# Transformer layers on one core: context loads ahead of weight stores, statistics moved a stage earlier, and a rounding shared with ScalarE

## What is computed

```python
x = x + _L0_ffn_ref(_layernorm(x, axis=-1), ...)            # 16 routed experts and a shared one
x = x + _L1_xattn_ref(_layernorm(x, axis=-1), ctx_2048, ...)  # attention, q and output in 8-bit steps
x = x + _L1_ffn_ref(_layernorm(x, axis=-1), gate_cp, up_cp, down_cp)
x = x + _L2_xattn_ref(_layernorm(x, axis=-1), ...)
x = x + _L2_ffn_ref(_layernorm(x, axis=-1), gate_w, up_w, down_w)

def _L1_ffn_ref(...):    # weights interpolated from control points
    w = 0.5 * (2.0 * p1 + (p2 - p0) * f + (...) * f2 + (...) * f3)
    inter = jax.nn.silu(gate) * up

def _mx_dequant(t):      # of L2_ffn, for activations and for each weight
    scales = jnp.maximum(max_abs / 448.0, 1e-30)              # per block of 32
    q = (blocks / scales[..., None]).astype(jnp.float8_e4m3fn).astype(jnp.float32)
    return (q * scales[..., None]).reshape(rows, feat)
```

## Time and profile before

| | |
|---|---|
| median of 3 runs | 2426.94 us (2417.49 to 2431.23) |
| profiled execution | 2430.76 us, span 2428.9 us |
| TensorE matmul busy | 2241.5 us (92% of the span) |
| VectorE / ScalarE / GpSimd busy | 1312.8 / 772.9 / 776.6 us |
| granted TensorE clock, mean | 0.954 |
| experts / second attention | about 684 to 956.6 / 956.7 to 1328.0 us |
| spline / column stage | 1328.0 to 1385.9 / 1385.9 to 1536.3 us |

### The profile page before, as it was taken

The page is one execution under the profiler, slowest core; times in us unless marked ns, Lnnn a source line. Parts: engine busy times, 40 slices in busy tenths (PEclk is TensorE's granted clock), DMA queues, the critical chain, the costliest instruction groups (busy, mean ns, idle before and its releaser), DMA issues. The chain is left out here.

```text
span 2428.9 us, 29430 instructions
## 1 busy us (share of the span) xinstructions
PE 2241.5 (92%) x10009; PEld 1185.2 (49%) x10009; DVE 1312.8 (54%) x3424; ACT 772.9 (32%) x2045; POOL 776.6 (32%) x784
## 2 busy tenths in 40 slices
PE   8999999998999997888886898799998899999899
PEld 4455555555455654444443454534443444444454
DVE  5544344106217656545555475776663355555897
ACT  1134344314011112434444311511110456645433
POOL 3655455203203214432232332400000365656100
PEclk9999999998999998989988799999999899999899
DMA  7025300005276864121111641520001211211000
GB/s 198 1 82 187 124 17 13 1 1 165 72 291 249 298 224 155 50 73 50 58 35 41 217 148 52 200 92 5 9 5 55 81 48 51 61 39 43 20 14 15
DMA packets 99802, 214.80 MB, mean 88 GB/s; under 512 B 19332, under 2 KB 40228, under 8 KB 97736
## 3 DMA queue, kind: packets, MB, share of 16 engines
q1 hardware_dynamic: 92232, 195.61, 23.7%
q0 software_dynamic: 7424, 17.32, 2.5%
HBM read 156.75 MB, written 51.18 MB: 86 GB/s over the span
## 5 line engine op out<-in xcount | busy, mean ns | idle before, releaser
L3864 POOL TENSOR_SCALAR a_p<-a_p,a_li 100x257 f32<-100x257 f32 x252 | 187.9, 763 | 110.7 <-DVE a_li L3727 110.7
L634 POOL TENSOR_SCALAR a_shared<-a_shared,a_li 128x361 f32<-128x361 f32 x104 | 131.5, 1265 | 182.4 <-DVE a_li L542 182.4
L3482 PE MATMUL bank<-l_early,a_ctx 128*128 128x512 f32 (+1 forms) x384 | 180.2, 615 | 0.0
L1590 PE MATMUL bank<-w_ctx,w_wk 128*128 128x361 f32 x256 | 101.6, 548 | 30.4 <-DMA w_ctx<-in_ctxT 29.8
L3482 PEld LDWEIGHTS bank<-l_early,a_ctx 128*128 128x128 f32 (+1 forms) x384 | 68.9, 189 | 85.0 <-issue 85.0
L314 PE MATMUL bank<-a_wk,a_ctx 128*128 128x512 f32 (+1 forms) x192 | 95.0, 615 | 9.6 <-DMA a_wk<-in_L_xattn_Wk 6.2
L2688 POOL TENSOR_TENSOR e_v<-e_triple,e_inv 128x768 f32<-128x768 f32 x20 | 33.1, 1654 | 206.7 <-DVE e_inv L2665 206.7
L692 ACT ACTIVATE a_shared<-a_shared,a_nm 128x361 f32<-128x361 f32 x104 | 62.1, 597 | 99.0 <-DVE a_nm L536 99.0
L2768 PE MATMUL bank<-f_h,s_w 128*128 128x400 f32 x256 | 92.1, 514 | 0.0
L314 PE MATMUL bank<-a_wv,a_ctx 128*128 128x512 f32 (+1 forms) x192 | 90.7, 592 | 0.0
L2418 ACT ACTIVATE f_sg<-bank 128x512 f32<-128x512 f32 x25 | 14.9, 597 | 237.4 <-PE bank L2201 221.7
(11 more groups left out here) (492 smaller groups left out, 4890.4 us busy)
## 6 DMA issues: line engine op xcount, KB each, us to landing
slots_x<-zero SPq DMA_DIRECT2D x4, 4096.0 KB, 27.0
s_whole<-in_L_ffn_w SPq DMA_DIRECT2D x24, 512.0 KB, 3.6
e_wg<-in_L_ffn_w_gate SPq DMA_DIRECT2D x16, 704.0 KB, 6.6
e_wu<-in_L_ffn_w_up SPq DMA_DIRECT2D x16, 704.0 KB, 8.2
e_wd<-in_L_ffn_w_down SPq DMA_DIRECT2D x16, 512.0 KB, 4.2
e_xg<-slots_x SPq DMA_DIRECT2D x16, 512.0 KB, 5.3
slots_y<-e_y SPq DMA_DIRECT2D x32, 256.0 KB, 4.5
a_ctx<-in_ctxT SPq DMA_DIRECT2D x30, 256.0 KB, 3.2
```

What stands on the lines that cost most here:

```text
L634: pool.tensor_scalar(p[s % NP], p[s % NP], li[:, b % 2, h:h + 1], None, ALU.mult).then_inc(normed, 1)
L1590: mm = nc.tensor.matmul(R.bank("k", b, n)[:, 0:T], wks[:, kc, n * P:(n + 1) * P], cx[b % 2][:, kc, :], start=(kc == 0), stop=(kc == KC - 1))
L3482: mm = nc.tensor.matmul(bank[0:m, :], columns[:, kc], w[:, kc, :], start=(kc == 0), stop=(kc == KC - 1))
L3864: pool.tensor_scalar(p[g % 2][j][:, lo:hi], p[g % 2][j][:, lo:hi], li[:, h, i:i + 1], None, ALU.mult) \
```

## The change

Four parts. In the second attention SP loads context and mask of b before it stores the spline weights of b - 2 and loads the taps of b; and the statistics that the spline stage needs are taken there, by VectorE behind each `add_output`, with the roots by GpSimd two sequences later (the last two in the spline stage). In the spline stage VectorE normalises all eight sequences first, into eight buffers; TensorE transposes four of them before the control point products and four behind them, with other banks. The experts round nine triples and the column stage seven, with three buffers, and not at n = 7. In the rounding VectorE masks the exponent ahead of the next half's scales (`power`), ScalarE makes of it the constant by a Relu with scale and bias (`lift`), and VectorE adds and subtracts in two scalar_tensor_tensor, which put back the offset.

```diff
+RAISE = 1.5 * 2.0 ** 20
...
-        self.half = self.sb("half", [P, 1])
+        self.half, self.lowest = self.sb("half", [P, 1]), self.sb("lowest", [P, 1])
...
@@ stage_L0_experts @@
-                triples.store(sp, EARLY_TRIPLES - 1)
...
                     copy_mid(u)
                     if u + 2 < U:
                         copy_x(u + 2)
+                    if u in ROUNDING_UNITS:
+                        triples.lift(act, ROUNDING_UNITS.index(u))
...
                         n = ROUNDING_UNITS.index(u)
+                        triples.power(dve, n)
                         if n + 1 < triples.n:
                             triples.scales(dve, step, n + 1)
                         triples.rounding(dve, step, n)
@@ stage_L1_attention @@
                 for b in range(2, B):
-                    store_weights(b - 2)
-                    load_taps(b)
                     sp.wait_ge(*R.full("v", b - 2, 2))
                     sp.wait_ge(multiplied, b - 1)
                     sp.dma_start(cx[b % 2][:], ctxT[b]).then_inc(c_in[b % 2], 16)
                     sp.wait_ge(maxed, (b - 1) * NH)
                     sp.dma_start(m_in[b % 2][:], mask[b]).then_inc(mk_in[b % 2], 16)
+                    store_weights(b - 2)
+                    load_taps(b)
...
+                def measure_next(b):
+                    step(dve.bn_stats(k.next_stats[:, b, :], k.res[:, b, :]))
+                    step(dve.bn_aggr(k.next_stat[:, b, :], k.next_stats[:, b, :]))
+                    dve.tensor_scalar(k.next_var[:, b:b + 1], k.next_stat[:, b, 1:2], LN_EPS, None, ALU.add) \
+                        .then_inc(next_var_made, 1)
...
                     if before:
                         add_output(b - 1)
+                        measure_next(b - 1)
...
                 add_output(B - 1)
+                measure_next(B - 1)
...
+                def next_root(b):
+                    pool.wait_ge(next_var_made, b + 1)
+                    pool.tensor_tensor(k.next_rstd[:, b:b + 1], k.next_var[:, b:b + 1], k.half[0:S, :], ALU.pow)
...
                     interpolate(b)
+                    if b >= 2:
+                        next_root(b - 2)
@@ constants @@
-EARLY_TRIPLES = 10
-ROUNDING_UNITS = [*range(4, 16), *range(24, 32)]
-STORES_AFTER = {t + 3 if t < 6 else t + 7: t for t in range(EARLY_TRIPLES - 1)}
+EARLY_TRIPLES = 9
+ROUNDING_UNITS = [*range(4, 16), *range(24, 30)]
+COLUMN_ROUNDINGS = [n for n in range(FC - 1) if n != FC // 2 - 1]
+STORES_AFTER = {t + 3 if t < 6 else t + 7: t for t in range(EARLY_TRIPLES)}
@@ class Triples @@
+    def power(self, dve, n):
+        dve.wait_ge(self.scaled, n + 1)
+        dve.tensor_scalar(self.c[n % 2][:].bitcast(I32), self.v[n % 2][:].bitcast(I32), EXPONENT, None, ALU.bitwise_and) \
+            .then_inc(self.power_taken, 1)
+
     def rounding(self, dve, step, n):
-        dve.wait_ge(self.scaled, n + 1)
+        dve.wait_ge(self.power_lifted, n + 1)
         a, p = self.v[n % 2][:], self.c[n % 2][:]
-        step(dve.tensor_scalar(p.bitcast(I32), a.bitcast(I32), EXPONENT, None, ALU.bitwise_and))
-        step(dve.tensor_scalar(p, p, 2.0 ** -6, 1.5 * 2.0 ** 20, ALU.max, ALU.mult))
-        step(dve.tensor_tensor(a, a, p, ALU.add))
-        dve.tensor_tensor(a, a, p, ALU.subtract).then_inc(self.v_rounded, 1)
+        step(dve.scalar_tensor_tensor(a, p, RAISE * 2.0 ** -6, a, ALU.add, ALU.add))
+        dve.scalar_tensor_tensor(a, a, RAISE * 2.0 ** -6, p, ALU.subtract, ALU.subtract).then_inc(self.v_rounded, 1)
+
+    def lift(self, act, n):
+        act.wait_ge(self.power_taken, n + 1)
+        p = self.c[n % 2][:]
+        act.activation(p, p, ACT.Relu, bias=self.k.lowest[:, 0:1], scale=RAISE).then_inc(self.power_lifted, 1)
@@ stage_columns_ffn @@
-        triples = Triples(k, ctx, tag, raw, rounded, EARLY_TRIPLES, FC, 2)
+        triples = Triples(k, ctx, tag, raw, rounded, EARLY_TRIPLES, FC, 3)
...
+                def gates(lo, hi):
+                    for m in range(lo, hi):
+                        silu(m)
+                        if (m - 3) / 2 in COLUMN_ROUNDINGS:
+                            triples.lift(act, COLUMN_ROUNDINGS.index((m - 3) // 2))
...
-                    if n < triples.n:
-                        if n + 1 < triples.n:
-                            triples.scales(dve, step, n + 1)
-                        triples.rounding(dve, step, n)
+                    if n in COLUMN_ROUNDINGS:
+                        i = COLUMN_ROUNDINGS.index(n)
+                        triples.power(dve, i)
+                        if i + 1 < triples.n:
+                            triples.scales(dve, step, i + 1)
+                        triples.rounding(dve, step, i)
@@ stage_L1_ffn @@
-            xn = [sb(f"xn{i}", [S, D]) for i in range(2)]
+            xn = [sb(f"xn{i}", [S, D]) for i in range(B)]
...
+            x_bank, sum_bank = lambda b: k.bank[(b + GB) % B], lambda half, v: k.bank[(QUADS * (half + 1) + v) % B]
...
+                    for b in range(GB):
+                        turn(b)
                     pe.wait_ge(c_in, 16)
                     for t in range(PARTS_W):
                         pe.wait_ge(multiplied, t + 1)
...
+                    for b in range(GB, B):
+                        pe.wait_ge(laid, (PARTS_W - 1) * N + b - GB + 1)
+                        turn(b)
                     pe.wait_ge(basis_in, 16)
                     for half in range(2):
+                        pe.wait_ge(xT_made, GB * (half + 1))
                         for v in range(QUADS):
-                            pe.wait_ge(xT_made, GB * (half + 1))
+                            if half == 0:
+                                pe.wait_ge(w_made, (PARTS_W - 1) * N + v + 1)
...
-                    for t in range(PARTS_W):
-                        measure(2 * t)
-                        measure(2 * t + 1)
-                        beyond_border(t)
                     for b in range(B):
                         normalize(b)
+                    for t in range(PARTS_W):
+                        beyond_border(t)
```

More of the change, by code:

```diff
@@ L553, in _ @@
                 dve.memset(k.ones[:], 1.0)
+                dve.memset(k.lowest[:], -RAISE * 2.0 ** -6)
                 dve.memset(k.res[:, B], 0.0)
@@ L2721, in _ @@
             def _(sp):
-                for t in range(2):
+                for t in range(3):
                     triples.load(sp, t)
@@ L2728, in _ @@
                     triples.stored(sp, t)
-                    if t + 2 < FC - EARLY_TRIPLES:
-                        triples.load(sp, t + 2)
+                    if t + 3 < FC - EARLY_TRIPLES:
+                        triples.load(sp, t + 3)
                 sp.wait_ge(early_in, 6 * 16)
@@ L2961, in _ @@
                 def _(pool):
-                    def root(b):
-                        pool.wait_ge(var_made, b + 1)
-                        pool.tensor_tensor(rstd[:, b:b + 1], var[:, b:b + 1], k.half[0:S, :], ALU.pow).then_inc(rstd_made, 1)
+                    pool.tensor_tensor(k.next_rstd[:, B - 2:B], k.next_var[:, B - 2:B], k.half[0:S, :].to_broadcast([S, 2]), ALU.pow) \
+                        .then_inc(rstd_made, 1)
                     for t in range(PARTS_W):
@@ L2978, in _, with turn @@
                 def _(pe):
+                    def turn(b):
+                        pe.wait_ge(xn_made, b + 1)
+                        for v in range(QUADS):
+                            mm = nc.tensor.transpose(x_bank(b)[:, v * S:(v + 1) * S], xn[b][:, v * P:(v + 1) * P], k.ident[0:S, 0:S])
+                        mm.then_inc(x_turned, 1)
+                    for b in range(GB):
+                        turn(b)
                     pe.wait_ge(c_in, 16)
@@ L2981, in _ @@
                         pe.wait_ge(multiplied, t + 1)
-                        for side, emptied in ((0, laid), (1, w_made)):
+                        for side in range(2):
                             for n in range(N):
                                 if t > 0:
-                                    pe.wait_ge(emptied, (t - 1) * N + n + 1)
+                                    pe.wait_ge((laid, w_made)[side], (t - 1) * N + n + 1)
+                                elif side == 1:
+                                    pe.wait_ge(xT_made, n + 1)
                                 rows = slice(32 * n, 32 * n + TERMS)
@@ L3006, in _, with copy_x @@
                 def _(act):
+                    def copy_x(b):
+                        act.wait_ge(x_turned, b + 1)
+                        act.copy(xT[:, :, b * S:(b + 1) * S], x_bank(b)[:, 0:QUADS * S].rearrange("p (v s) -> p v s", v=QUADS)) \
+                            .then_inc(xT_made, 1)
+                    for b in range(GB):
+                        copy_x(b)
                     for t in range(PARTS_W):
@@ L3010, in _ @@
                             act.copy(wd[:, t * N + n, :], k.bank[n][:]).then_inc(laid, 1)
-                    for b in range(B):
-                        act.wait_ge(x_turned, b + 1)
```

(17 more changed lines are left out.)

40 lines of the change are left out of this document (15 added, 25 removed).

## The result

The kernel after takes 2358.84 us (median of 4 executions, 2352.34 to 2362.94), the kernel before beside it 2428.05 (2417.49 to 2431.23): ratio 0.972, 95% interval 0.9683 to 0.9757. The forecast was 2363, in a range of 2345 to 2395. In what follows, products are cold where they run at the 1.2 GHz level of TensorE's clock, the hole is TensorE's idle time at n = 7 of the column stage, and the pitch is the time from one of its steps n to the next.

What follows compares the result with a forecast made beforehand. TensorE was taken as the bound, so its waits were counted: attention -40.8, spline -9.5, experts -7.5, columns -7.5, together -65.3 us, from the median 2426.94 to 2361.7, stated as 2363, range 2345 to 2395.

Steps and rivals of the forecast that it cites:

- SP's order: Second attention: loading context and mask first removes six waits, -29.8 us, and slow-clock key products, -14.0 us.
- New stalls: Second attention: GpSimd stops VectorE's quantising, delaying maxima 2 to 4 us; charged +2 us, ends 0 and +24.
- rivals 1 and 5: Second attention: another wait takes half the gain, 2383, chance 0.15; GpSimd stops quantising chains, 2467, chance 0.03.
- measure_next, 1.05 us: Second attention: three added VectorE steps per sequence, hidden seven times, bare after the last sequence: +1.05 us.
- Spline stage, -9.5: Spline stage: without statistics and with early transposes, basis products start at 25.1 us instead of 34.5; ends -6 and -15.
- Experts, -7.5: Experts' end: nine triples let the stage end at 949.2 instead of 956.66; cheaper rounding worth nothing; ends -6 and -8.5.
- Column stage, -7.5: Column stage: shorter iterations -1.05, no rounding at n = 7 -5.5, clock behind it -1.0; ends -4 and -9.
- it ends as before: Column stage, first iteration: power(0) waits for GpSimd ahead of scales(1), yet the iteration ends no later.
- rival 3: Column stage: two-input steps stopped beside GpSimd, VectorE's iteration 7.6 us at worst, +7, 2370; chance 0.09.
- double sign of being wrong: Column stage: wrong if two-input steps take over 1.5 us beside GpSimd and the iterations grow.
- The lift: ScalarE's rounding step: 0.9 to 1.03 us each, with no table load between, at no cost.
- rival 4: Experts: each lift needs two table loads, 2.6 us, costing 1 us x 18, hidden in the columns: 2381; chance 0.03.

Runs made afterwards that it cites:

- e1: Kernel before with SP's order alone (context and mask loaded ahead of the weights' store and taps): 2380.38 us against 2422.42.
- e4: Kernel after with the four old rounding steps on VectorE and no lift on ScalarE: 2357.88 us, ratio 0.9733 to the kernel before.
- e2: Kernel after with SP's old order, all else kept: 2404.65 us, ratio 0.9926 to the kernel before.
- e6: Kernel after with the column stage's rounding at n = 7 kept: 2363.23 us, ratio 0.975 to the kernel before.
- e5: Kernel after run again unchanged: ratio 0.9749 to the kernel before.
- e7: Kernel after with ten triples in the experts and six in the column stage: ratio 0.9764 to the kernel before.
- e9: Kernel after with e8's edits and the scaling of the sixth layer's bias moved from n = 1 to n = 3: ratio 0.9719 to the kernel before.
- e10: Kernel after with the column stage's third triple loaded behind the sixth layer's tensors: 2363.73 us, ratio 0.9745 to the kernel before.
- e11: The kernel of e9 run once more: ratio 0.9727 to the kernel before.
- e12: Kernel after run a third time, unchanged: ratio 0.9735 to the kernel before.
- e3: Kernel before with only the statistics in the attention and the reordered spline stage: 2421.50 us against 2422.42.
- e8: Kernel after, column stage: GpSimd scales behind four gathers instead of eight, VectorE makes half 1's scales before the first power: 2355.99 us, ratio 0.9731.

## Why the prediction held, point by point

The mechanisms held; that the sum came so near is in part luck, since errors of both signs offset each other. The second attention gained more (46.3) and the column stage less (3.2) than the outer end that each was given (45 and 4).

- **SP's order.** The mechanism was right, and both terms were too small. The waits were costed at 29.8 and the clock at 14.0; alone, the order took 32.6 us of idle time and 16.3 of busy time from the stage. I had counted only the waits for the context and only the products of the keys: 2.2 us of waits for ScalarE's copies of the probabilities went too, and other products behind each wait had been cold as well. The term's own ends, -45 and -20, don't follow from its parts either: with 0 and 24 for new stalls they add to -42.75 and -18.75.
- **New stalls, charged with 2 us.** VectorE was stopped as foretold and more: in `tokens`, the first wide tensor_scalar of the quantising (L1415) has a median of 2.61 us and a maximum of 3.25 in the kernel after (0.49 before), and with the one behind it (1.38 instead of 0.43) a chain is 3 to 4 us late. In one sequence the normalising itself was held as long as two GpSimd instructions took, 4.42 us instead of 0.54:

```profile
1055.44 4.42 DVE L1782 TENSOR_SCALAR a_xn<-res,a_stat,a_rstd 100x512 f32<-100x512 f32 x1
1055.48 1.12 POOL L1912 TENSOR_SCALAR w_mask<-w_mask 100x361 f32<-100x361 f32 x1
1056.58 2.99 POOL L1957 TENSOR_TENSOR a_prod<-w_ctx,a_row_weights 128x1444 f32<-128x1444 f32 x1
```

  TensorE did not wait for it once: the waits L1647, L1611 and the rest are those of before. The charge should have been nothing, as its lower end said; rivals 1 and 5 fell with it.
- **measure_next, 1.05 us.** Mis-sized. The attention is 2.6 us longer with the statistics than in e1. The stage's end shows 0.9 (from the last `add_output` to the next stage 3.27 us instead of 2.34), and two waits for ScalarE's key copies, 1.6 us, stand in the kernel after and not in e1. The steps that were called hidden seven times are not quite.
- **Spline stage, -9.5.** It was -11.3. The start at 5.3 us and the transposes (3.25 and 2.93 for two times 1.70) were right. The parts were put at 4.1 us each; without the statistics between GpSimd's products four of them take 15.35.
- **Experts, -7.5.** It was 7.2 in the profiled pair without the earlier drift, and 7.4 over all traces. The cheaper rounding is worth nothing there, as e4 shows.
- **Column stage, -7.5.** Here the sum was too large for the kernel after (-3.2), though not for e2 with the same stage (-7.4). Leaving out the rounding at n = 7 gave 5.5 us of hole, as forecast, and 5.9 in all by e6. Of the 1.05 us for six shorter iterations 0.6 were gained, from the fourth step to the eighth, but the third and fourth come 0.2 and 1.6 us later than before, and "it ends as before" was only true of the third. TensorE waits 3.69 us ahead of it instead of 1.57, and the products behind run at the low clock; so the stage is 0.95 us behind at the eighth. The 1.0 us of clock behind the hole were 0.3 in the kernel after and all 1.96 in e2. And 1.7 us of cold products behind the projection stood in no row of the kernel before; that term was missing. The sum by the trace is +0.95 + 1.7 - 5.55 - 0.3 = -3.2. The prediction had said that without idle time nothing lowers the clock; that held in the attention (1.00 over 130 us), but not here.
- **The port, rival 3.** Its mechanism is there: 1.15 us more for the second two-input step of a pair (not the first, as the rival had it), 0.5 for the exponent's mask where it meets GpSimd. The Trainium skill (GPSIMD Engine Reference, 1. Specifications) names contention for VectorE instructions with two SBUF inputs; the trace agrees, with 2.11 against 0.96 us. VectorE's iteration is 6.3 to 6.5 us (its products start at 1349.48, 1355.82 and 1362.27), where I had said 5.6 and the rival 7.6, and that stays below TensorE's 7.12. So the port costs nothing here. Of the double sign of being wrong, steps of over 1.5 us and longer iterations, only the first came.
- **The lift.** 0.93 us in ScalarE, within the forecast's 0.9 to 1.03, and no table load between lifts. The Trainium skill (ScalarE: Activation LUTs, Table sets: the hidden batching unit) says that relu is in every set; the trace agrees, and rival 4 fell.
- **The sum** came out 3.3 us short of the profiled pair's 68.6 because what was missed in the attention (5.5), the spline stage (1.8) and ahead of the attention (1.8, no more than the earlier drift of 2.1) was mostly offset by the column stage (-4.3) and the rest (-1.5).

## What to carry to other kernels

Where a queue serves two consumers, look at what its in-order waits tie together: here a load that TensorE was waiting for stood behind a store that waited for the slowest producer, and putting it first was worth more than all other edits together. Cost a removed wait by the whole stage's busy time, not by the one product behind it, since every product until the clock is back ran cold. And where a stage's clock falls at fixed places, an edit of a microsecond upstream can bring or take several: judge a small edit by the steps up to the first fall, and look at the clock before calling the rest its effect.

## What the runs showed of the hardware

- The granted clock can fall while TensorE has no idle time in the records. Behind 32 products of 8 columns it was 0.57 over 4 us in the kernel after, and the 16 products there took 7.31 us in e5, e6, e7, e9 to e12 as well and 8.12 in e1, where the clock fell during the 32 already; behind the same 32 products they took 5.62 in the kernel before, e2, e3, e4 and e8. What decides it stays open: the kernels differ in where this step lies and in what was idle before, and no run varied the one without the other.
- Where it falls in the column stage is nearly the same in each execution of a kernel: the stage took 147.13, 147.07 and 147.14 us in one kernel, 143.38 and 143.46 in another. It is not so for the whole program: behind that stage the latter kernel took 890.95 and 899.06 us, with TensorE busy for 836.22 and 842.71.
- A scalar_tensor_tensor of 128x768 with two SBUF inputs takes 0.96 us alone and 2.11 where it starts during a GpSimd tensor_tensor of that size; one that starts 0.16 us ahead of it keeps 0.90, and the GpSimd instruction goes from 1.50 to 2.06. A tensor_scalar of 100x512 was stopped for up to 3.9 us (0.54 to 4.42), across two GpSimd instructions.
